# A token tower with a mixture of experts on one core: the loop over sequences 1 to 4, rolled or written out

## The reference

```python
h = tok(x)                      # 64 columns gathered, 64 from a softmax over 64 clusters
h = h + attn(layernorm(h))      # decayed linear attention without softmax, then a gelu operator
h = h + ffn(layernorm(h))       # router, top 6 of 64 experts, capacity, SwiGLU experts, 2 shared ones
```

## Time and profile before

| | us |
|---|---|
| runs, median (lowest, highest) | 737.2 (735.7, 737.61) |
| the profiled execution | 738.8 |
| its span, first to last instruction | 736.7 |
| TensorE busy | 688.4 |
| VectorE, GpSimd, ScalarE busy | 524.2, 463.3, 350.2 |
| mean granted TensorE clock | 0.961 |

### The profile page before, as it was taken

One profiled execution on the slowest core, in us unless ns is written; L12 is line 12 of the kernel. 1 busy time (PEld: TensorE's weight loads), 2 busy tenths in 40 slices (PEclk: granted clock), 3 DMA queues, 4 the chain that ended last, 5 costly groups with the idle time before them and its releaser, 6 DMA issues.

```text
span 736.7 us, 10995 instructions
## 1 busy us (share of the span) xinstructions
PE 688.4 (93%) x2943; PEld 514.8 (70%) x2943; DVE 524.2 (71%) x1073; ACT 350.2 (48%) x607; POOL 463.3 (63%) x349
## 2 busy tenths in 40 slices
PE   4547899999999999988999999999999999999997
PEld 3426677777777777766777777777777777777775
DVE  4478867887769868757678877698677865774443
ACT  3333374545553474533745455543745445534432
POOL 5013667675676766656676756767676657576664
PEclk8556999999999999999999999999999999999999
DMA  5501332333333433323333333333334424334441
GB/s 209 208 1 51 113 101 93 121 106 104 116 100 103 120 103 108 118 86 106 103 97 120 108 100 114 101 110 116 111 101 116 121 86 119 109 108 130 138 121 57
DMA packets 48859, 80.17 MB, mean 109 GB/s; under 512 B 9504, under 2 KB 13728, under 8 KB 48800
## 3 DMA queue, kind: packets, MB, share of 16 engines
q1 hardware_dynamic: 47776, 77.44, 33.3%
q0 software_dynamic: 1024, 2.10, 1.4%
HBM read 76.35 MB, written 3.15 MB: 108 GB/s over the span
## 4 chain that ended last, share of the span: by engine, by line
PE 87%; DVE 5%; issue 3%; POOL 1%; ACT 1%; DVEq 0%; POOLq 0%
PE bank_y L472 15%; PE bank_g L486 8%; PE bank_u L488 8%; PE bank_u L486 8%; PE bank_g L487 8%; PE bank_u L487 8%; PE bank_g L488 8%; PE bank_y L467 4%; PE bank_y L466 4%; PE bank_y L469 4%; PE bank_f L391 1%; PE bank_f L383 1%; PE bank_f L407 1%; PE bank_f L424 1%; PE bank_f L413 1%
## 5 line engine op out<-in xcount | busy, mean ns | idle before, releaser
L1019 POOL TENSOR_TENSOR hid<-hid,gate_rows 128x512 f32<-128x512 f32 x256 | 372.1, 1462 | 195.1 <-DVE hid L861 193.3
L609 ACT ACTIVATE hid<-bank_g 128x512 f32<-128x512 f32 x264 | 156.7, 599 | 276.1 <-PE bank_g L488 274.1
L861 DVE TENSOR_TENSOR hid<-hid,bank_u 128x512 f32<-128x512 f32 x264 | 178.9, 682 | 133.2 <-PE bank_u L488 74.8
L486 PE MATMUL bank_g<-x_hi,gate_hi 128*128 128x512 f32 x264 | 144.3, 546 | 0.0
L472 PE MATMUL bank_y<-hid,w_down 128*128 128x512 f32 x272 | 138.9, 592 | 0.0
L867 DVE TENSOR_TENSOR hid_lo<-hid,hid_hi 128x512 fp32r<-128x512 f32 x128 | 111.1, 868 | 4.5 <-ACT hid_hi L615 4.3
L487 PE MATMUL bank_g<-x_hi,gate_lo 128*128 128x512 f32 x264 | 105.7, 400 | 0.0
L486 PE MATMUL bank_u<-x_hi,up_hi 128*128 128x512 f32 x264 | 105.4, 399 | 0.0
L488 PE MATMUL bank_u<-x_lo,up_hi 128*128 128x512 f32 x264 | 105.4, 399 | 0.0
L488 PE MATMUL bank_g<-x_lo,gate_hi 128*128 128x512 f32 x264 | 105.3, 399 | 0.0
L487 PE MATMUL bank_u<-x_hi,up_lo 128*128 128x512 f32 x264 | 105.0, 398 | 0.0
(11 more groups left out here) (201 smaller groups left out, 829.7 us busy)
## 6 DMA issues: line engine op xcount, KB each, us to landing
gate_rows<-gates_dram SPq DMA_DIRECT2D x512, 128.0 KB
w_down<-down_t_dram SPq DMA_DIRECT2D x3, 704.0 KB, 13.8
out_dram<-later SPq DMA_DIRECT2D x8, 256.0 KB, 3.0
hid<-gate_t_dram SPq DMA_DIRECT2D x2, 704.0 KB, 5.6
gates_dram<-gates_t SPq DMA_DIRECT2D x8, 128.0 KB, 2.3
gate_rows<-up_t_dram SPq DMA_DIRECT2D x1, 704.0 KB, 5.5
later<-up_t_dram SPq DMA_DIRECT2D x1, 704.0 KB, 8.3
raw<-gate_t_dram SPq DMA_DIRECT2D x1, 704.0 KB, 9.4
```

What stands on the lines that cost most here:

```text
L486: pe.matmul(o, w_hi[name][:, p, :], x3_hi[par][:, :], start=True, stop=False)
L609: act.activation(hid[:, slot(par, p), :], bank_g[(p + par) % 2][:, :], ACT.Silu).then_inc(sem("silu"), 1)
L861: dve.tensor_tensor(hid[:, s, :], hid[:, s, :], bank_u[(p + par) % 2][:, :], ALU.mult)\
L1019: pool.tensor_tensor(hid[:, s, :], hid[:, s, :], gate_rows[:, row, :], ALU.mult)\
```

## The change

`sequences` becomes a Python loop, so that all eight sequences are written out on all five engines. b is a plain number everywhere: each wait has a constant, each DMA a constant address, the gather reads `idx` directly, and `idx_now`, its copy and the two waits around the copy are gone. Lines behind the change have lower numbers by 7 to 21.

```diff
         def wait(eng, name, value):
 
-            if isinstance(value, int) and value <= 0:
+            if value <= 0:
                 return
             eng.wait_ge(sem(name), value)
 
         def sequences(eng, one):
-
-
-            one(0, 0, True, True)
-            with eng.Fori(0, (BATCHES - 4) // 2) as i:
-                one(i * 2 + 1, 1, True, True, i + 2)
-                one(i * 2 + 2, 0, True, True, i + 3)
-            one(BATCHES - 3, 1, True, True, (BATCHES - 1) // 2 + 1)
-            one(BATCHES - 2, 0, True, False)
-            one(BATCHES - 1, 1, False, False)
+            for b in range(BATCHES):
+                one(b, b % 2, b < BATCHES - 1, b < BATCHES - 2)
...
             sp.wait_ge(sem("gates_t"), b + 1)
-            dst = gates_dram[b] if isinstance(b, int) else \
-                gates_dram[bass.ds(b, 1), :, :].rearrange("a e s -> (a e) s")
-            sp.dma_start(dst, gates_t[:, :]).then_inc(sem("gates_stored"), 16)
+            sp.dma_start(gates_dram[b], gates_t[:, :]).then_inc(sem("gates_stored"), 16)
...
-        def gather(pool, b, par, t, prev_use):
-
-            if isinstance(b, int):
-                at = idx[:, b * TILES + t:b * TILES + t + 1]
-            else:
-                at = idx_now[:, t:t + 1]
+        def gather(pool, b, par, t):
+
+            at = idx[:, b * TILES + t:b * TILES + t + 1]
             if t == 0:
 
                 wait(pool, "hx", b - 1)
-                if not isinstance(b, int):
-
-                    pool.wait_ge(sem(f"gathered{1 - par}"), 16 * TILES * prev_use)
-                    pool.tensor_copy(idx_now[:, :], idx[:, bass.ds(b * TILES, TILES)]).then_inc(sem("idx_now"), 1)
-                    pool.wait_ge(sem("idx_now"), b - 2)
                 alone(pool, "pool_passed")
             pool.indirect_dma_start(emb[par][:, t, :], None, table[:, :],
                                     bass.IndirectOffsetOnAxis(ap=at, axis=0)).then_inc(sem(f"gathered{par}"), 16)
```

More of the change, by code:

```diff
@@ L194, in build @@
         taken_end = sb("taken_end", [EXPERTS, 1])
-        idx_now = sb("idx_now", [P, TILES], I32)
         taken = sb("taken", [EXPERTS, SEQ])
@@ L292, in gate_row_loads @@
                 sp.wait_ge(sem("gates_stored"), 16 * b + 16)
-                if isinstance(b, int) and b == 0:
+                if b == 0:
                     staging_free(sp, "rows")
@@ L296, in gate_row_loads @@
                 sp.wait_ge(sem("gated"), PAIRS * b + r + 1 - GATE_RING + 1)
-            elif not (isinstance(b, int) and b == 0):
+            elif b:
                 sp.wait_ge(sem("gated"), PAIRS * b + r + 1 - GATE_RING)
-            src = gates_dram[b, 2 * r:2 * r + 2, :] if isinstance(b, int) else \
-                gates_dram[bass.ds(b, 1), 2 * r:2 * r + 2, :].rearrange("a e s -> (a e) s")
+            src = gates_dram[b, 2 * r:2 * r + 2, :]
             for k in range(2):
@@ L303, in gate_row_loads, with sync_sequence @@
                              src[k:k + 1, :].to_broadcast([F, SEQ])).then_inc(sem(f"gate_rows{row}"), 16)
-        def sync_sequence(sp, b, par, late, early, use=0):
+        def sync_sequence(sp, b, par, late, early):
             for p in range(PAIRS):
@@ L308, in sync_sequence @@
                     gate_row_loads(sp, b, p - 1)
-                if p == STORE_AT and not (isinstance(b, int) and b == 0):
+                if p == STORE_AT and b:
                     store(sp, b - 1)
@@ L315, in store_gates @@
             sp.wait_ge(sem("gates_t"), b + 1)
-            dst = gates_dram[b] if isinstance(b, int) else \
-                gates_dram[bass.ds(b, 1), :, :].rearrange("a e s -> (a e) s")
-            sp.dma_start(dst, gates_t[:, :]).then_inc(sem("gates_stored"), 16)
+            sp.dma_start(gates_dram[b], gates_t[:, :]).then_inc(sem("gates_stored"), 16)
         def store(sp, b):
             sp.wait_ge(sem("result"), b + 1)
-            dst = out_v[b] if isinstance(b, int) else \
-                out_v[bass.ds(b, 1), :, :, :].rearrange("a p t d -> (a p) t d")
-            sp.dma_start(dst, result[:, :, :]).then_inc(sem("stored"), 16)
+            sp.dma_start(out_v[b], result[:, :, :]).then_inc(sem("stored"), 16)
         @block.sync
@@ L456, in down @@
             q = PAIRS * b + p
-            if isinstance(b, int) and b == 0 and p == 0:
+            if b == 0 and p == 0:
                 pe.wait_ge(sem("w_down"), 16 * (PAIRS // CHUNK))
@@ L461, in down @@
             if is_split(p):
-                if isinstance(b, int) and b == 0 and p == 1:
+                if b == 0 and p == 1:
                     pe.wait_ge(sem("down_lo"), 1)
@@ L477, in gate_up @@
             q = PAIRS * b + p
-            if isinstance(b, int) and b == 0 and p % CHUNK == 0:
+            if b == 0 and p % CHUNK == 0:
                 for n in ("gate", "up"):
@@ L496, in pe_out, with pe_sequence @@
             last.then_inc(sem("pe_out"), 1)
-        def pe_sequence(pe, b, par, late, early, use=0):
-            first = isinstance(b, int) and b == 0
+        def pe_sequence(pe, b, par, late, early):
+            first = b == 0
             for p in range(PAIRS):
@@ L605, in act_silu @@
             act.wait_ge(sem("pe_gate"), q + 1)
-            if isinstance(b, int) and b == 0 and p in (0, RING // 2):
+            if b == 0 and p in (0, RING // 2):
                 staging_free(act, "hid1" if p else "hid0")
@@ L620, in act_copy_out, with act_sequence @@
             act.activation(ffn_t, bank_y[par][:, :], ACT.Copy).then_inc(sem("ffn_t"), 1)
-        def act_sequence(act, b, par, late, early, use=0):
-            first = isinstance(b, int) and b == 0
+        def act_sequence(act, b, par, late, early):
+            first = b == 0
             for p in range(PAIRS):
@@ L873, in dve_out, with dve_sequence @@
             dve.tensor_tensor(result[:, :, :], tiles(bank_f[0]), h2[par][:, :, :], ALU.add).then_inc(sem("result"), 1)
-        def dve_sequence(dve, b, par, late, early, use=2):
-            first = isinstance(b, int) and b == 0
+        def dve_sequence(dve, b, par, late, early):
+            first = b == 0
             for p in range(PAIRS):
@@ L882, in dve_sequence @@
                 if early:
-                    dve_early(dve, b + 2, par, p, use)
+                    dve_early(dve, b + 2, par, p, b // 2 + 2)
                 if first:
@@ L1001, in pool_early, with pool_sequence @@
                                    ALU.pow).then_inc(sem("inv1"), 1)
-        def pool_sequence(pool, b, par, late, early, use=0):
+        def pool_sequence(pool, b, par, late, early):
             for p in range(PAIRS):
@@ L1009, in pool_sequence @@
                     if p in GATHER_AT:
-                        gather(pool, b + 2, par, GATHER_AT.index(p), use if par else use - 1)
+                        gather(pool, b + 2, par, GATHER_AT.index(p))
                 q = PAIRS * b + p
@@ L1038, in _ @@
             for t in range(TILES):
-                gather(pool, 0, 0, t, 0)
+                gather(pool, 0, 0, t)
             pool.wait_ge(sem("halves"), 1)
             for t in range(TILES):
-                gather(pool, 1, 1, t, 0)
+                gather(pool, 1, 1, t)
             for p in range(PAIRS):
```

## The result

The change takes 728.9 us (median of 4 runs, 728.14 to 729.25) where the kernel before takes 737.4 (4 runs, 735.7 to 738.23): ratio 0.9887, 95% interval 0.9874 to 0.9901, 8.5 us less. The forecast was 728.5, 8.71 less.

A forecast was written before the change was run, and what follows sets the result against it. TensorE bounds the kernel (busy 688.4 of 736.7 us), so control code wins only where an upstream engine is late: 5.19 + 3.12 + 0.40 = 8.71 us, from 737.2 to 728.5 us; range for 8 in 10: 726.5 to 731.3.

The forecast's parts named there:

- The jump's lateness: VectorE at the loop's single jump back, between sequences 2 and 3: idle 4.94 us on "issue", making it 3.64 us late.
- The rival that the stall isn't the jump's: VectorE's code arrives late whatever leads to it, so the 4.94 us stall and its clock stay: 733.7 us; 5%.
- the prediction's last sentence on fetching: Instruction cache has two lines of 256 instructions; the jump's stall would be a first line that has to be fetched again.
- The clock behind it: TensorE after its idle times at the jump: granted clock 0.50 for 3.4 us, L383 to L413 takes 1.56 us longer.
- half clock was an accident: Half clock behind the jump stays or was chance: gain 7.15 us, 730.1 us; counted with the forecast, together 84%.
- The copy: GpSimd's index copy delays the first gather and TensorE's state matmuls by 0.78 us; four copies, 3.12 us.
- The register wait: VectorE's wait for gates_stored between scan and gate step: 0.10 us into each of sequences 2 to 5, 0.40 us.
- SyncE and code fetch: SyncE's registers and DMA addresses gain nothing; some 6 more code packets on queue 8 cost 0, bounds 0 and 21.8 us.
- the sum: All gains together: 5.19 us for the jump with its clock, 3.12 for copies, 0.40 for register waits: 8.71 us.

## Why the prediction was right

*The jump's lateness, 3.63 us: right.* With VectorE alone in its loop the interval is 3.61 longer (86.94 - 83.33); with a hint on it the lateness is gone. The prediction laid it to the jump from the idle row alone. What it is was open: a fetch, on three engines at once, two in a row on VectorE, and hidden on the others. The branch itself takes 0.06 us on VectorE. The rival that the stall isn't the jump's is out. The blocks of 256 instructions that the prediction's last sentence on fetching works with are TensorE's; VectorE's packets are half as long.

*The clock behind it, 1.56: right for the trace, too regular.* It is 1.56 where the spell of half clock falls behind TensorE's second wait (the kernel before; 88.93 - 84.11 = 4.82 in the variant with one instruction more, so 1.2), and 0 where it falls into the stretch that VectorE's lateness covers. The rival "half clock was an accident" is half right. That it did no harm to the forecast is in part luck: the spell was in the one trace read, and how many executions of the kernel before have it where it costs isn't known (with VectorE's hint alone the medians show some 0.8 us of it). The change has no half clock between 88 us and the last matmuls.

*The copy, 0.78 each: right,* measured alone (84.0 against 83.22), in four sequences.

*The register wait, 0.10: right,* measured alone (83.33 against 83.22, scan to gate step 1.41 against 1.31).

*SyncE and code fetch, nothing: right here.* 5 more packets on queue 8, 6 forecast, in intervals that don't differ by more than 0.02. They are TensorE's: with TensorE in its loop queue 8 is back at 18. The other engines' code comes by queue 14, which the prediction didn't count.

Against the kernels that run at the rate of before, the five intervals gained 0.79, 0.90, 6.07, 0.90 and 0.12 (84.00, 84.12, 89.31, 84.11 and 83.33, less 83.21 to 83.24): 8.78, where the sum had 8.71. One sentence was wrong: after the change TensorE would idle some 0.3 us before the state matmuls. It was 0.40, with TensorE's faster rate in that trace as the likely reason; in the variants with ScalarE's or TensorE's loop it is 0.25 to 0.28. The span, forecast at 728.0, was 726.3, and some 1.2 us of that is the same rate (0.15 us in each of eight sequences).

## What to carry to other kernels

Look first for a place where the kernel already does the same work without the thing to be removed: here one straight-line sequence beside the loop gave every term to 0.1 us. The idle time on "issue" right behind the backward branch was a fetch of code, and a hint on that one engine's back edge won the most of it back without writing anything out; the rest here was mostly a 0.18 us copy that the loop forced, which cost 0.78 each time by its wait. An operation moved on GpSimd moves the products behind it too: look which VectorE operations with both inputs in SBUF then come to wait for one.

## What the runs showed of the hardware

- At one and the same jump back ScalarE, SyncE and VectorE stood 2.5, 2.8 and 3.4 us until the first instruction of the next pass, TensorE and GpSimd 0.4 and 0.3. Padding ScalarE's pass from 320 to 452 instructions didn't change its fetch (2.5, 2.4). Slack decides which is felt, and VectorE stood 2.7 us a second time.
- In straight code TensorE fetched 16 KB for each 251 executed instructions (queue 8), the other four engines 8 KB for each 126 (queue 14).
- Hints on all five loops brought a stall of 1.19 us on ScalarE behind a table load, 65 us after the loops had ended. The hint on VectorE alone didn't. The cause is open.
- Two traces can differ by 0.2% in TensorE's rate at a granted clock of 1.00 (80.87 us in four kernels, 81.02 in ten, for the same matmuls), and idle times before a wait then differ by some 0.12 us. What sets the rate is open.
- VectorE operations with both inputs in SBUF waited for two-input operations of GpSimd and ended 0.55 to 0.56 us (`hid_lo`, 128x512) or 0.29 to 0.30 us (128x256) after them. With an indirect gather just ahead of such a GpSimd product they took 2.38 us in place of 0.80 and 1.65 in place of 0.45; L848, with one input in PSUM, was never stretched.
